# A graph layer's gathers and its products on TensorE: visits cut at every second chunk, a mixer spread over two pairs

## The reference, cut to what matters

```python
xn = _layernorm(x, axis=-1)                                  # 12500 rows of 256
x = x + gnn(xn) + mix(xn)
x = x + ffn(_layernorm(x, axis=-1))

def gcn_conv(x, W, b, src, dst, num_nodes):                  # twice: 256->128 with relu, 128->256
    h = x @ W
    ...                                                      # self loops added: 212500 + 12500 edges
    msg = h[s] * norm[:, None]
    out = jax.ops.segment_sum(msg, d, num_segments=num_nodes)
    return out + b

def mix(feature):                                            # a lambda layer with batch norm
    QK = einsum('bnd,kde->bkne', feature, W_qk) + b_qk
    value = einsum('bnd,de->bne', feature, W_v) + b_v
    lam = einsum('bnd,bne->bde', softmax(QK[:, 1], axis=1), value)
    ...                                                      # lam normalised per row
    return einsum('bnd,bde->bne', QK[:, 0], bn)

def ffn(x):                                                  # top half of the rows by a router weight
    h = gelu(x @ w1 + b1)                                    # 256 -> 1024
    y = (h @ w2 + b2) * weight                               # 1024 -> 256
    return x with y added at the selected rows
```

## Time and profile before

| | |
|---|---|
| median of 3 runs | 5297.94 us (5284.9 to 5299.58) |
| profiled execution | 5290.04 us, its span 5288.1 us |
| busy, share of the span | POOL 3259.5 us (62%), PE 2871.2 (54%), DVE 1749.5 (33%), ACT 1219.3 (23%) |
| gathers (line 492) | 3328, 3145.3 us busy, 1761.2 us idle before them |
| mean granted clock of TensorE | 0.729 |

### The profile page before, as it was taken

One profiled execution on the slowest core, in us unless ns is written; L12 is line 12 of the kernel. 1 busy time (PEld: TensorE's weight loads), 2 busy tenths in 40 slices (PEclk: granted clock), 3 DMA queues, 4 the chain that ended last, 5 costly groups with the idle time before them and its releaser, 6 DMA issues.

```text
span 5288.1 us, 59794 instructions
## 1 busy us (share of the span) xinstructions
PE 2871.2 (54%) x16358; PEld 2463.6 (47%) x16359; DVE 1749.5 (33%) x4541; ACT 1219.3 (23%) x2622; POOL 3259.5 (62%) x3493
## 2 busy tenths in 40 slices
PE   6634444444444444344327667667667776675773
PEld 5533333333333333333326656656556655565662
DVE  8522222222222222222213333323333333333336
ACT  3411111111111111111003323323323332332331
POOL 3566666666666666666656666666666666666650
PEclk7866666666666666666667888878878877888886
DMA  4211111111111111111121111111111111111116
GB/s 117 67 47 48 49 47 48 48 48 48 47 49 48 47 49 48 48 48 48 49 58 49 50 48 50 50 48 49 50 49 49 50 49 49 49 50 48 50 45 197
DMA packets 191366, 288.61 MB, mean 55 GB/s; under 512 B 59596, under 2 KB 137588, under 8 KB 191094
## 3 DMA queue, kind: packets, MB, share of 16 engines
q0 software_dynamic: 106496, 218.32, 15.9%
q1 hardware_dynamic: 83572, 68.55, 4.2%
q10 hardware_dynamic: 1232, 1.05, 0.1%
HBM read 249.19 MB, written 38.49 MB: 54 GB/s over the span
## 4 chain that ended last, share of the span: by engine, by line
another core or an unknown queue 33%; issue 25%; PE 21%; ACT 12%; DVE 6%; DVEq 1%; POOL 0%; ACTq 0%; DMA 0%; SPq 0%; POOLq 0%
PE bank L741 5%; PE bank L879 4%; PE bank L786 4%; PE bank L889 3%; ACT arena L620 2%; PE bank L865 1%; DVE arena L1172 1%; ACT arena L590 1%; DVE arena L1035 1%; ACT L609 1%; ACT L620 1%; ACT L614 1%; ACT L583 1%; PE bank L863 1%
## 5 line engine op out<-in xcount | busy, mean ns | idle before, releaser
L492 POOL DMA_INDIRECT arena<-table,idx_now x3328 | 3145.3, 945 | 1761.2 <-issue 901.8
L741 PE MATMUL bank<-arena 128*128 128x128 f32 x6656 | 1037.6, 320 | 186.5 <-issue 69.6
L741 PEld LDWEIGHTS bank<-arena 128*128 128x128 f32 x6656 | 1001.3, 235 | 216.7 <-issue 116.7
L1183 DVE SCALAR_TENSOR_TENSOR acc<-bank,from_base,acc 128x128 f32 x416 | 146.0, 351 | 2100.0 <-remote 1598.5
L889 PE MATMUL bank<-arena 128*128 128x256 f32 x1568 | 499.9, 476 | 317.5 <-ACT arena L620 263.3
L879 PE MATMUL bank<-arena 128*128 128x128 f32 x3136 | 499.1, 334 | 213.5 <-ACT arena L616 205.9
L879 PEld LDWEIGHTS bank<-arena 128*128 128x128 f32 x3136 | 480.5, 246 | 237.4 <-ACT arena L616 228.2
L1172 DVE SCALAR_TENSOR_TENSOR arena<-dst_of,base_col,bank 128x1024 f32 (+1 forms) x416 | 532.5, 1280 | 96.0 <-DVE acc L1183 84.1
L889 PEld LDWEIGHTS bank<-arena 128*128 128x128 f32 x1568 | 356.7, 238 | 411.4 <-ACT arena L620 294.4
L780 PE MATMUL bank<-ident,arena 128*128 128x128 f32 x196 | 67.2, 446 | 710.3 <-ACT arena L590 451.8
L786 PE MATMUL bank<-arena 128*128 128x256 f32 x392 | 203.3, 674 | 419.9 <-ACT arena L594 419.9
(11 more groups left out here) (245 smaller groups left out, 3027.5 us busy)
## 6 DMA issues: line engine op xcount, KB each, us to landing
arena<-table,idx_now POOLq DMA_INDIRECT x3328
base_rows<-arena SPq DMA_DIRECT2D x98, 128.0 KB
xs<-in_x_dram SPq DMA_DIRECT2D x6, 1792.0 KB, 16.4
acc<-base_rows SPq DMA_DIRECT2D x9, 896.0 KB, 10.2
out_dram<-acc SPq DMA_DIRECT2D x8, 896.0 KB, 8.1
table<-acc SPq DMA_DIRECT2D x7, 896.0 KB, 4.7
table<-acc SPq DMA_DIRECT2D x98, 64.0 KB
arena<-base_rows SPq DMA_DIRECT2D x5, 896.0 KB, 11.8
```

The lines of the kernel that those rows point to most:

```text
L492: pool.indirect_dma_start(ring[:, quarter * HALF + k, :], None, table[layer], bass.IndirectOffsetOnAxis(ap=idx_now[:, gg % 2, c:c + 1], ax ...
L741: last = nc.tensor.matmul(visit_sum[h][:, 0:F], S[:, h, k, :], ring[:, quarter * HALF + k, :], start=(k == 0), stop=(k == HALF - 1))
L1183: last = dve.scalar_tensor_tensor(a, visit_sum[h][:, 0:F], mask[:, ds(turn, 1)], a, ALU.mult, ALU.add)
```

## The change

Four things change.

1. **PE waits for gathers by two chunks.** Each quarter has four semaphores, one for two chunks, shared by both layers; `sum_half` waits ahead of every second chunk.
2. **Other products stand between the chunks of a visit.** `sum_half` takes a table from chunk to a step that is run ahead of it.
3. **The mixer of layer 1 is spread over two pairs.** In the pair of tile t stand its transposes and keys; its exponentials' transposes and its sums stand in the pair after. xn has two buffers and is written by VectorE at the end of the pair before. Two more small buffers hold the factors and totals. The first two pairs and one last are written out.
4. **The feed-forward steps of layer 2 stand inside the visits**, the down and hidden products cut in halves.

```diff
-        s_gath = [[sem(f"gathered{i}_{h}") for h in range(4)] for i in range(2)]
+        s_gath = [[sem(f"gathered{h}_{k}") for k in range(HALF // 2)] for h in range(4)]
@@ gpsimd
-                                ).then_inc(s_gath[layer][quarter], 16)
+                                ).then_inc(s_gath[quarter][k // 2], 16)
@@ scalar
-            def mix(t, n):
-
-                act.wait_ge(s_mG, t + 1)
-                act.activation(xn, xs[:, ds(t, 1), :].rearrange("p a d -> p (a d)"), ACT.Identity,
-                               bias=nmr[:, ds(t, 1)], scale=rstd[:, ds(t, 1)]).then_inc(s_mxn, 1)
+            def mix(t, of, n):
+                factor, total = factors[of], totals[of]
+
                 act.wait_ge(s_mT, t + 1)
...
@@ tensor
-            def sum_half(h, quarter):
+            def sum_half(h, quarter, gg1, before):
                 for k in range(HALF):
+                    if k in before:
+                        before[k]()
+                    if k % 2 == 0:
+                        pe.wait_ge(s_gath[quarter][k // 2], gg1)
                     last = nc.tensor.matmul(visit_sum[h][:, 0:F], S[:, h, k, :], ring[:, quarter * HALF + k, :],
                                             start=(k == 0), stop=(k == HALF - 1))
...
-            def mix_3(t):
+            def mix_3(t, xn, first):
                 pe.wait_ge(s_mEe, t + 1)
+                if not first:
+                    pe.wait_ge(s_mu, t)
...
+                first_half, second_half = {}, {}
+                if ends:
+                    first_half[2] = lambda: mix_2(g - 1)
+                    second_half[6] = lambda: mix_3(g - 1, xn2[:, 1 - par, :], first)
+                if begins:
+                    first_half[4] = lambda: mix_1(g, xn2[:, par, :])
+                    second_half[0] = lambda: mix_keys(g, 0)
+                    second_half[2] = lambda: mix_keys(g, 1)
+                visit(0, gg1, g1, 2 * par, first_half)
+                visit(0, gg1, g1, 2 * par + 1, second_half)
...
-                    visit(1, gg1, g1, 2 * par)
-                    with pe.If(f1 > 0):
-                        ff_3(t1)
-                    with pe.If(f0 > 0):
-                        ff_1(t0)
-                        ff_mixed(t0)
-                    visit(1, gg1, g1, 2 * par + 1)
-                    with pe.If(f0 > 0):
-                        ff_2(t0)
-                        ff_hidden(t0)
+                    visit(1, gg1, g1, 2 * par,
+                          {1: lambda: of_tile(f1, ff_3, t1, 0), 4: lambda: of_tile(f1, ff_3, t1, 1),
+                           6: lambda: of_tile(f0, ff_1, t0)})
+                    visit(1, gg1, g1, 2 * par + 1,
+                          {0: lambda: of_tile(f0, ff_mixed, t0), 4: lambda: of_tile(f0, ff_2, t0),
+                           6: lambda: of_tile(f0, ff_hidden, t0, 0)})
+                    of_tile(f0, ff_hidden, t0, 1)
@@ vector
+            def mix_xn(t, of):
+                dve.tensor_scalar(xn2[:, of, :], xs[:, ds(t, 1), :].rearrange("p a d -> p (a d)"), rstd[:, ds(t, 1)],
+                                  nmr[:, ds(t, 1)], ALU.mult, ALU.add).then_inc(s_mxn, 1)
...
+                if before:
+                    mix_3(g - 1, 1 - par)
+                if after:
+                    mix_xn(g + 1, 1 - par)
```

More of the change, by code:

```diff
@@ L594, in mix @@
                 act.activation(En.rearrange("p k n -> p (k n)"), pE[:, 0:D], ACT.Copy).then_inc(s_mEe, 1)
-            with act.Fori(0, TILES - 1) as t:
-                mix(t, P)
-            mix(TILES - 1, LAST)
+            with act.Fori(0, TILES // 2 - 1) as m:
+                for of in range(2):
+                    mix(m * 2 + of, of, P)
+            mix(TILES - 2, 0, P)
+            mix(TILES - 1, 1, LAST)
             for i, (dsts, srcs) in enumerate(((GT, pT), (WqT, pK))):
@@ L743, in sum_half, with visit @@
                 return last
-            def visit(layer, gg1, g1, quarter):
+            def visit(layer, gg1, g1, quarter, before):
                 h = quarter % 2
-                pe.wait_ge(s_gath[layer][quarter], gg1)
                 pe.wait_ge(s_S[layer][h], g1)
-                sum_half(h, quarter).then_inc(s_sum[layer][h], 1)
+                sum_half(h, quarter, gg1, before).then_inc(s_sum[layer][h], 1)
             def extra_visits(layer, gg1, g, par, word):
@@ L767, in mix_1, with mix_keys @@
                 last.then_inc(s_mT, 1)
-            def mix_keys(t):
-                pe.wait_ge(s_mTe, t + 1)
-                for e in range(KD):
-                    for k in range(KD):
-                        last = nc.tensor.matmul(pK[:, e * P:(e + 1) * P], Wk[:, k, e * P:(e + 1) * P], xT[:, k, :],
-                                                start=(k == 0), stop=(k == KD - 1))
-                last.then_inc(s_mK, 1)
+            def mix_keys(t, e):
+                if e == 0:
+                    pe.wait_ge(s_mTe, t + 1)
+                for k in range(KD):
+                    last = nc.tensor.matmul(pK[:, e * P:(e + 1) * P], Wk[:, k, e * P:(e + 1) * P], xT[:, k, :],
+                                            start=(k == 0), stop=(k == KD - 1))
+                if e == KD - 1:
+                    last.then_inc(s_mK, 1)
             def mix_2(t):
@@ L831, in _ @@
             last.then_inc(s_m1, 1)
-            for par in range(2):
-                pair_of_layer_1(TILES // 2, par, False)
+            pair_of_layer_1(TILES // 2, 1, False, False)
             pe.wait_ge(s_m3, 3)
@@ L873, in ff_2, with ff_hidden @@
                 last.then_inc(s_lT, 1)
-            def ff_hidden(t):
-                pe.wait_ge(s_lTe, t + 1)
-                for h in range(KH):
+            def ff_hidden(t, half):
+                if half == 0:
+                    pe.wait_ge(s_lTe, t + 1)
+                for h in range(half * (KH // 2), (half + 1) * (KH // 2)):
                     for k in range(KD):
@@ L883, in ff_hidden, with ff_3 @@
                         last.then_inc(s_h, 1)
-            def ff_3(t):
-                for h in range(KH):
-                    if h % (KH // 2) == 0:
-                        pe.wait_ge(s_H, t * 2 + (h // (KH // 2) + 1))
+            def ff_3(t, half):
+                pe.wait_ge(s_H, t * 2 + (half + 1))
+                for h in range(half * (KH // 2), (half + 1) * (KH // 2)):
                     last = nc.tensor.matmul(pY[:, 0:D], H[:, h, :], fw2[:, h, :], start=(h == 0), stop=(h == KH - 1))
-                last.then_inc(s_y, 1)
+                if half == 1:
+                    last.then_inc(s_y, 1)
             with pe.Fori(0, PAIRS // 2) as gg:
@@ L1261, in pair_of_layer_1 @@
                     finish_layer_1(t0)
-                if before is not None:
-                    mix_3(before)
                 add_main(0, 0, at_places[0], g3)
@@ L1273, in pair_of_layer_1 @@
                     build_main(0, g1, 1, turns[1])
+                if before:
+                    mix_3(g - 1, 1 - par)
+                if after:
+                    mix_xn(g + 1, 1 - par)
             first_builds(0)
[L1276 to L1283 removed]
+            mix_xn(0, 0)
+            pair_of_layer_1(0, 0, n=P, after=True)
+            with dve.Fori(0, TILES // 2 - 1) as m:
+                for par in (1, 0):
+                    pair_of_layer_1(m * 2 + (2 - par), par, n=P, before=True, after=True)
+            pair_of_layer_1(TILES - 1, 1, n=LAST, before=True)
+            pair_of_layer_1(TILES, 0, before=True)
             dve.wait_ge(s_mu, TILES)
```

83 lines of the change are left out of this document (36 added, 47 removed).

## The result

The changed kernel takes 5255.6 us (5252.9 to 5264.9), the one before 5295.6 us on the same chip: a ratio of 0.9933 (95% 0.992 to 0.9945). That is 40 us, where I had forecast 255. The profiled execution took 5264.94 us, 25 us less than that of before. From the gathers' starts: layer 1's stage lasts 2382.0 us instead of 2407.9, layer 2's 2469.3 instead of 2478.0, the first gather starts 11 us later, 2 us are added between the layers, and the end is 4 us shorter.

The account below looks back on a forecast made before the run. The prediction took GpSimd's gathers, waiting at ring halves that PE releases late, to bound the kernel. 5290 less 154 (layer 1) and 98 (layer 2) gave 5038, stated as 5040 us; the range was 4640 to 5440.

Parts of the forecast that it names:

- some 740 us of the 5290 us are at stake: Both gather stages: GpSimd's waits for ring halves PE releases late, 345 us in layer 1 and 418 us in layer 2.
- The floor that I used, 1.25 us: GpSimd, both layers: a gather takes 0.945 us, the next starts 0.30 us later, so 16 chunks take at least 20.0 us.
- PE finishes a long dense run slowly, and catches up when GpSimd stands still: Visits in both layers: beside gathers, matmuls start 1.4 us apart; after the last gather a visit takes 1.95 us.
- Three quarters of 2.1 us: Layer 1, PE's idle time ahead of the transposes of xn: 1.6 us a pair saved, 154 us over 96 pairs.
- what is late next: Layer 1: a loop through VectorE, with the next xn queued behind late keys; so not the whole 2.1 us is taken.
- the copy on VectorE: Layer 1, writing xn: about 0.45 us beside other work; uncovered it would be 44 us.
- the table load: Layer 1, ScalarE: goes or moves ahead of the copy of xT, between -1.28 and +1.28 us a pair.
- Layer 2, 98 us: Feed-forward steps inside visits: net gain of 1.4 us a pair, taken as 1.0 us, over 98 pairs with a tile.
- The 0.8 us that I set down for ScalarE's copy: Layer 2, idle time ahead of the hidden products: about 0.8 us for ScalarE's copy, counted as covered by the change.
- Rival 2: Nothing follows: PE's results come only when GpSimd pauses, whatever their order; time stays 5290 us (5274 to 5306); chance 0.15.
- Rival 1: The waits vanish: short matmul runs are never slowed, PE keeps up and GpSimd runs through; 4560 us; chance 0.15.
- Rivals 3 and 4: Layer 2 slower: first visit tied to the feed-forward chain, 5390 us, chance 0.22; PE's clock falls, 5410 us, chance 0.06.

Follow-up runs that it names:

- e1: Kernel before, with one product in each visit instead of eight; selection matrices, gathers and waits stay: 5315.6 us against 5325.9, a ratio of 0.9973.
- e2: Kernel before, with gathers of 128 bytes a row instead of 512, as many gathers and rows: a ratio of 1.0003.
- e15: Kernel before in five stretches: layer 1 with mixer, then visits alone with one product, then eight; layer 2 in changed order, then order before: ratio 0.9936.
- e17: Layer 1 in the changed order, layer 2 in the order before, with 16 gathers a pair, then 12: a ratio of 0.9382 to the kernel before.
- e16: Kernel before, by stretches of 26 pairs: memsets after each gather, extra plain transfers, or gathers of 96 or 64 rows: a ratio of 1.0314.
- e9: The changed kernel, unaltered, against the kernel before on a chip of the second kind: a ratio of 0.9995.
- e4: Kernel before, with a small memset on GpSimd after every gather, waited for before the next gather: a ratio of 1.0228.
- e3: Kernel before, with each gather replaced by a plain transfer of 128 neighbouring rows, 64 KB as before, issued by GpSimd: 3169.2 us, a ratio of 0.5951.

## Why the prediction was wrong

**"So some 740 us of the 5290 us are at stake. They lie in GpSimd's waits for PE".** This step failed. The waits are there, but PE's work was not their cause. On a chip of the first kind a gather takes, on average over a stretch, 1.43 to 1.52 us in every kernel with GpSimd at its own step (before, after, e1, e2, e15 to e17), with 4 to 88 matmul records a pair, with and without work on ScalarE. 16 of them are 23.2 us in layer 1 and 23.9 in layer 2; GpSimd issues them in 20.0 and stands still for the rest. The floor that I used, 1.25 us, is GpSimd's own and holds only on chips of the second kind, where the kernel takes 4552 us. No row of before excluded a floor of 1.45 us. One pair of rows hinted at it: GpSimd's idle time is nearly the same in both layers, though PE has 3637 matmul records in 1000 us of layer 2 and 2064 in as much of layer 1.

**"PE finishes a long dense run slowly, and catches up when GpSimd stands still."** True as a sight, wrong as a cause. The earlier trace rows show steps of 1.4 us on PE; e1 and e15 show the same steps on VectorE. My reading made dense runs the fault, and cutting them the cure; spread over the gathers the same products were 12.3 us late instead of 12.2.

**"Three quarters of 2.1 us", 154 us.** The stage gained 25.9 us, 0.26 us a pair: this term was to be held wrong below 60 us, and it is. The 2.1 us of PE's idle time became 7.2 us, since xn now waits on VectorE behind the late addition, as "what is late next" had named. The small terms held: the copy on VectorE took 0.41 us (I had 0.45) and lies beside other work; the table load went to the copy of xT, once in two pairs (22 for 43 tiles). Why 0.26 us remain is not shown; e17 has the same pair of 22.9 us, with layer 2's order as before.

**Layer 2, 98 us.** 8.7 us by the two traces, and none in e15, where the changed order has 1.51 us a gather and the order before 1.50. The order covered what it was to cover, and the idle time came back ahead of the mixed rows: 189.0 us for 39 tiles are 4.8 us a tile, where it was 0.94. The 0.8 us that I set down for ScalarE's copy stands in no row; the copy itself is 0.38 us.

**The rivals.** Rival 2, "nothing follows", came nearest: 5274 to 5306 against 5264.9 in the profiled execution. I gave it 0.15 and should have given it most, since its row for, a release two to four us after the last gather in both layers and never elsewhere, does not depend on PE's order. Its reason, that PE's results come only when GpSimd pauses, fell with e15 and e16. Rival 1, 4560 us, is what a chip of the second kind does, before the change as well as after it (4554.0 and 4553.3 us), so it was no effect of the change. Rivals 3 and 4 did not come: layer 2's pair is 23.86 us, the clock 0.83. The direction and the range were right, but that the time lies in the range says little for the forecast, since the range took in rival 2. The sum, 5038 and 8 us for the median, should have read 5046 and not 5040. As to the start, the 11 us by which the first gather starts later are not the change's, since e9, the same kernel, has it at 238.0 us (before 234.7, after 245.8).

**Still open:** what is shared and full, why chips differ, why the price moves between 1.43 and 1.54 us (layer 2 of e4), and why PE and not VectorE is usually the late one. No run on a chip of the first kind lets GpSimd go on without waiting for the ring, so it isn't shown whether gathers could then be issued every 1.25 us throughout.

## What to carry to other kernels

When an engine waits at a ring for another, don't take the other for the cause: give it almost nothing to do in one run and see whether the pause goes. Divide a stage by the count of the operation that it is made of; a quotient that stays nearly the same in layers with different work (1.45 and 1.49 us a gather here) hints at a price of that operation. Here only fewer gathers (e17) or plain transfers in their place (e3) made the kernel much shorter. And time a kernel with gathers on several chips before its waits are read.

## What the runs showed of the hardware

- Indirect gathers of 128 rows issued every 1.25 us cost 1.43 to 1.52 us each on at least four chips and 1.25 us on two; the kernel before takes 5290 to 5331 us on the former and 4551 to 4554 us on the latter, 14% less.
- On those of the first kind, while gathers run, instructions of PE, VectorE and SyncE advance at times in steps of 0.70 us or twice that, up to 9 us after the last gather (e15). No register instruction of VectorE or SyncE takes 0.6 us or more with plain transfers of the same bytes (e3), with gathers 1.8 us apart (e16) or on chips of the second kind, and none of ScalarE's does in the kernel before, e1 and e15. VectorE's addition takes 349 to 351 ns with and without the steps.
- The cost is the same for 128, 96 and 64 rows (1.49 to 1.50 us, e16) and for 512 and 128 bytes a row (e2, a ratio of 1.0003).
- A gather that starts some 0.15 us into VectorE's write of xn takes 1.06 to 1.08 us instead of 0.94 (76 in the kernel after, 77 in e17; in e9, where the two meet in this way once, one).
- PE's records pass on as if nothing were late; only the waits of others show it. The Trainium skill (Perfetto Trace Analysis, "Summary: the profiler window per engine type") says that the end of a TensorE instruction is estimated and the true one hidden. The traces agree, and show by how much a record can run ahead: in the kernel after, PE's records of both visits are over by 2013.85 us and GpSimd is released at 2026.12 us. Whether the starts or only the ends of these records are early they don't tell.
